# The passage between two layers of a graph network: where the last chunk but one accumulates, when its h is taken, and when the self weights are loaded

## What is computed

```python
def _layer(h, e_h, src, dst, iso_mask, norm, W_r, W_sl, W_el):
    self_msg = jnp.where(iso_mask[:, None], h @ W_el, h @ W_sl)
    msg = (e_h + h[src]) @ W_r
    agg = segment_sum(msg, dst, num_segments=h.shape[0])
    return rrelu(agg * norm + self_msg)

h = relu(layernorm(x))
for W_r, W_sl, W_el in [(W_r1, W_sl1, W_el1), (W_r2, W_sl2, W_el2)]:
    h = _layer(h, e_h, src, dst, iso_mask, norm, W_r, W_sl, W_el)
x = x + h          # then a second layernorm, qk = h @ Wqk, and attention along the edges
```

## Time and profile before

| | |
|---|---|
| runs | 801.25 us median of 3 (798.9 to 801.87) |
| profiled execution | 801.75 us, its span 800.0 us |
| PE busy | 721.3 us (90%) |
| DVE, ACT, POOL busy | 515.8, 430.2, 239.1 us |
| chain that ended last | PE 68%, DVE 9%, DMA 7%, ACT 6%, issue 6% |
| mean granted clock of PE | 0.925 |

### The profile page before, as it was taken

One profiled execution on the slowest core, in us unless ns is written; L12 is line 12 of the kernel. 1 busy time (PEld: TensorE's weight loads), 2 busy tenths in 40 slices (PEclk: granted clock), 3 DMA queues, 4 the chain that ended last, 5 costly groups with the idle time before them and its releaser, 6 DMA issues.

```text
span 800.0 us, 15458 instructions
## 1 busy us (share of the span) xinstructions
PE 721.3 (90%) x5799; PEld 537.1 (67%) x5799; DVE 515.8 (64%) x932; ACT 430.2 (54%) x1085; POOL 239.1 (30%) x272
## 2 busy tenths in 40 slices
PE   3566699989899999988999999899999999999995
PEld 2545588879899998877988999544444444444455
DVE  5798999978788777441333333433665757565667
ACT  0557566756466656562111111477676767677671
POOL 7200000000000222210000000256665766666663
PEclk6555589999999999999999999999999999999997
DMA  4102000032310000101222111210000000000000
GB/s 131 45 7 60 17 2 8 13 104 71 98 45 8 8 8 8 43 30 56 65 87 75 38 38 35 89 47 0 1 15 12 13 13 14 13 14 13 4 24 20
DMA packets 39763, 27.89 MB, mean 35 GB/s; under 512 B 5311, under 2 KB 38163, under 8 KB 39686
## 3 DMA queue, kind: packets, MB, share of 16 engines
q1 hardware_dynamic: 38514, 25.89, 11.2%
q10 hardware_dynamic: 1172, 0.98, 0.4%
HBM read 13.28 MB, written 10.80 MB: 30 GB/s over the span
## 4 chain that ended last, share of the span: by engine, by line
PE 68%; DVE 9%; DMA 7%; ACT 6%; issue 6%; SPq 2%; ACTq 1%; POOL 1%; POOLq 0%; DVEq 0%
PE sums L1492 16%; PE sums L1475 15%; PE sums L1013 12%; PE sums L1086 8%; PE sums L1052 8%; DVE work L842 2%; ACT counts L1268 2%; DMA h_attention<-work 2%; DMA work<-in_x 2%; SPq L554 2%; DVE work L836 2%; PE sums L1020 1%; DMA counts<-in_x 1%; PE sums L1109 1%; PE sums L1027 1%
## 5 line engine op out<-in xcount | busy, mean ns | idle before, releaser
L1571 POOL TENSOR_TENSOR counts<-counts,work 125x500 f32<-125x500 f32 x150 | 165.4, 1102 | 95.5 <-DVE work L1632 88.4
L1052 PE MATMUL sums<-work 125*128 125x196 f16 (+15 forms) x1220 | 154.9, 253 | 20.4 <-DVE work L842 20.3
L1632 DVE SCALAR_TENSOR_TENSOR work<-sums,counts 125x500 f32<-125x500 f32 x150 | 101.7, 678 | 105.4 <-ACT sums L1589 105.4
L1492 PE MATMUL sums<-work 125*128 125x500 f32 (+1 forms) x350 | 159.0, 544 | 7.5 <-DVE work L1632 4.5
L1475 PE MATMUL sums<-work 128*125 128x500 f32 x300 | 150.5, 583 | 0.0
L1584 ACT ACTIVATE sums<-sums,work 125x500 f32<-125x500 f32 (+1 forms) x157 | 102.0, 650 | 75.3 <-PE sums L1475 72.0
L836 DVE TENSOR_TENSOR work<-work,counts 125x3024 f16<-125x3024 f16 (+1 forms) x60 | 114.3, 1905 | 35.9 <-PE sums L1054 32.5
L1268 ACT CAST counts<-sums 128x364 f32 (+38 forms) x305 | 131.3, 471 | 2.5 <-issue 0.6
L1054 PE MATMUL sums<-work 125*128 125x10 f16 (+15 forms) x800 | 132.0, 194 | 0.0
L842 DVE TENSOR_TENSOR work<-work,counts 125x4200 f16<-125x4200 f16 (+15 forms) x120 | 125.5, 1085 | 0.0
L1013 PE MATMUL sums<-counts 125*128 125x250 f16 (+1 forms) x975 | 121.6, 269 | 3.4 <-ACT work L1200 3.2
(11 more groups left out here) (177 smaller groups left out, 687.7 us busy)
## 6 DMA issues: line engine op xcount, KB each, us to landing
first_columns<-counts SPq DMA_DIRECT2D x5, 610.4 KB
counts<-first_columns SPq DMA_DIRECT2D x5, 610.4 KB
counts<-counts SPq DMA_DIRECT2D x5, 468.8 KB
counts<-in_x SPq DMA_DIRECT2D x5, 312.5 KB
h_nodes<-counts SPq DMA_DIRECT2D x5, 312.5 KB
work<-in_x SPq DMA_DIRECT2D x12, 125.0 KB
x_after_messages<-work SPq DMA_DIRECT2D x12, 125.0 KB
h_attention<-work SPq DMA_DIRECT2D x12, 125.0 KB
```

Of the source, the lines that this page charges most:

```text
L1052: pe.matmul(win[:, 0:c, cols], lo[:, k * 2 * LO:k * 2 * LO + 128], m[:, k, h0 * w:(h0 + c) * w].rearrange("p (h d) -> p h d", d=w), start= ...
L1492: last = pe.matmul(ps_o[c % 2][:, 0:cols(u) // n], h3[:, source(c, j + i), :], pbuf[u % PB][:, i * NP:i * NP + cols(u) // n], start=j + i ...
L1571: pool.tensor_tensor(a, a, p, ALU.add).then_inc(acc_done, 1)
L1632: dve.scalar_tensor_tensor(pbuf[u % PB], ps_s[u % 4][0:NP, 0:WIDE], float(np.exp(-CLIP)), counts[0:NP, source(c, j), target(c) * WIDE:(tar ...
```

## The change

Three edits.

1. Chunk 11 accumulates in banks 4 and 5 (those of group 197) in place of 2 and 3 (those of group 199). PE's own 11 waits for `put` of 2 * 198, which is groups 0 to 197, and no longer for all 200 groups.
2. ACT's own 11 stands ahead of the drain of group 199, and no longer behind it.
3. The two halves of `ws` are issued on ACT behind rest 12, ahead of split 6 and the branch. `wr` stays behind the branch and behind `agg_done`, and ACT first waits there until both halves of `ws` have landed. PE waits for `ws` alone ahead of layer two's first self matmuls, and for `wr` behind them.

The other lines belong to the second path, which the flag skips for these inputs: it must leave the self weights of layer one or two in place when it has run.

```diff
-    banks1 = lambda c: (psum[:, 2, :], psum[:, 3, :]) if c == DIRECT + 1 else (psum[:, 6, :], psum[:, 7, :])
+    banks1 = lambda c: (psum[:, 4, :], psum[:, 5, :]) if c == DIRECT + 1 else (psum[:, 6, :], psum[:, 7, :])
...
-                    pe.wait_ge(put, 2 * READY[c] if c <= DIRECT else 2 * GROUPS)
+                    pe.wait_ge(put, 2 * max(READY[c], GROUPS - 2) if c == DIRECT + 1 else 2 * READY[c])
...
             def weigh(i, c):
                 if i == 0:
-                    pe.wait_ge(L["wts"], 16 * 3)
+                    pe.wait_ge(L["wts"], 16 * 2)
                 pe.wait_ge(L["turned_out"], i + 1)
...
                 last.then_inc(L["self"], 1)
+                if i == 0:
+                    pe.wait_ge(L["wts"], 16 * 3)
                 pe.wait_ge(L["summed_out"], i + 1)
...
                     if kind in ("own", "self", "rest"):
                         layer1(kind, q)
+                if g == GROUPS - 1:
+                    layer1("own", DIRECT + 1)
                 c = reach(g)
...
-            layer1("own", DIRECT + 1)
             split(0, 0)
...
             layer1("rest", LAST)
+            for t, v in zip((ws[:, 0:D], ws[:, D:]), weights2[1:]):
+                act.dma_start(t, v).then_inc(L["wts"], 16)
             split(6, 0)
...
             act.wait_ge(agg_done, CHUNKS)
-            for t, v in zip((wr, ws[:, 0:D], ws[:, D:]), weights2):
-                act.dma_start(t, v).then_inc(L["wts"], 16)
+            act.wait_ge(L["wts"], 16 * 2)
+            act.dma_start(wr, weights2[0]).then_inc(L["wts"], 16)
```

More of the change, by code:

```diff
@@ L384, in again_sp @@
         sp.dma_start(hn[0:NP, :], h_dram).then_inc(R["hn_in"], 16)
+        sp.wait_ge(L["wts"], 16 * 2)
+        for t, v in zip((ws[:, 0:D], ws[:, D:]), weights1[1:]):
+            sp.dma_start(t, v).then_inc(R["edges"], 16)
     def again_pool(pool):
@@ L467, in again_dve @@
         dve.memset(zeros_r, 0.0).then_inc(R["begin"], 1)
-        dve.wait_ge(R["edges"], 48)
+        dve.wait_ge(R["edges"], 80)
         dve.wait_ge(R["ramp"], 1)
@@ L598, in _ @@
                 sp.dma_start(heads.rearrange("p (j d) -> p j d", d=HEAD), counts[0:NP, 0:NB, 0:HEAD]).then_inc(R["heads"], 16)
-                sp.wait_ge(R["heads"], 16)
+                for t, v in zip((ws[:, 0:D], ws[:, D:]), weights2[1:]):
+                    sp.dma_start(t, v).then_inc(R["heads"], 16)
+                sp.wait_ge(R["heads"], 48)
             sp.wait_ge(put, 2 * GROUPS)
@@ L1137, in _ @@
                 again_pe(pe)
+                pe.wait_ge(R["heads"], 48)
                 own(0, ORDER2[0])
```

## The result

| | before | changed |
|---|---|---|
| median of 11 runs | 801.87 us (798.75 to 807.9) | 795.57 us (790.71 to 797.56) |
| profiled execution | 801.75 us | 796.59 us |
| its span | 800.0 us | 794.8 us |

The ratio is 0.9912, 95% interval 0.989 to 0.9934: 5.3 to 8.8 us faster; the two medians are 6.3 us apart. The forecast was 794.0 with a range of 791.5 to 797.8, faster by more than 0.5% with a chance of 0.85.

A forecast was written before the change was run, and what follows sets the result against it. The prediction took PE, running with no gap ahead of the passage and from layer two on, as the bound. 2.0 + 1.7 + 2.2 + 1.9 = 7.8 us off 801.75 gave 794.0 us, range 791.5 to 797.8.

The forecast's parts named there:

- the 75 sums start earlier: Chunk 11's sums on PE start at 343.2 in place of 345.19: 2.0 us won, bounds 1.6 to 2.1.
- they run at full clock: Chunk 11's 75 sums no longer run at the lower clock: 1.7 us won, bounds 0 and 1.8.
- the branch's idle: PE's idle from 366.8 to 368.45, at the branch over the second path, was counted as the branch's and unchanged.
- L1109 without its wait: PE's wait for the last weight half ahead of L1109 goes: 2.2 us won, bounds 0.3 and 2.25.
- first round at full clock: Layer two's first round, L1109 to L1099, no longer runs at the lower clock: 1.9 us won, bounds 0 and 1.9.
- The first place: Around own 11, edits 1 and 2: sums start 2.0 us earlier and run 1.7 us faster at full clock.
- The second place: Ahead of L1109, edit 3: 2.2 us of idle go and the first round gains 1.9 us at full clock.
- the clause on contention: Weight DMAs took 2.7, 3.6 and 5.8 us to land because SP's loads of x and `first_columns` run beside them.
- The rule against the row: A compare-and-branch takes about 108 ns by the skill, so some 1.5 us of PE's idle there would be no branch.
- The rivals: Clock falls all the same (0.18), a wait turns into another (0.10), change does not do what it says (0.04), slower (0.03).
- The store of h for attention: Its landing should precede the next load of x: slack 3.4 us against 2.9 us; if not, up to 1.5 us return.
- the third rival: Own 11 still starts late because of a wait hidden behind the drain; 4.1 of 7.8 us left, 797.9; chance 0.04.

The follow-up runs named there:

- e3: Kernel before with only chunk 11's banks and PE's shorter wait changed; ACT's order and the weight loads as before: 801.18 us, ratio 0.9972.
- e4: Kernel before with 25 unused matmuls added ahead of own 11 and 20 ahead of layer two's first weigh: 800.34 us, ratio 0.9962.
- e7: Kernel before, with SP holding back its first large load of `first_columns` until layer two's three weights have landed: 798.91 us, ratio 0.996.
- e5: Changed kernel without PE's branch and PE's part of the second path: 792.28 us, ratio 0.9881.
- e6: Changed kernel with turned h of chunks 11 and 12 in their second bank, sums not waiting for ACT's copy, agg behind the first sums: 790.77 us.
- e8: The changed kernel, unedited, timed and profiled once more on another chip: 792.37 us, ratio 0.9897.
- e10: Changed kernel without the weight-load lines that the change adds to SP's unused second path: 797.12 us, ratio 0.9906.
- e9: Kernel before plus only the weight-load lines that the change adds to SP's unused second path: 802.03 us, ratio 0.9973.
- e1: Changed kernel with the weight loads put back as before, keeping the new banks and ACT's order: 799.28 us, ratio 0.9961.
- e2: Kernel before with only the earlier loading of the two `ws` halves; banks and own 11 as before: 796.19 us, ratio 0.9929.

## Why the prediction was right, and where it was off

By its own steps, from before's profile to the changed one's, in the order of the passage:

| step | forecast, us | measured, us |
|---|---|---|
| the 75 sums start earlier | 2.0 | 2.16 |
| they run at full clock | 1.7 | 1.67 |
| the branch's idle | 0 | 0.34 |
| L1109 without its wait | 2.2 | 2.41 |
| first round at full clock | 1.9 | 1.77 |
| sum | 7.8 | 8.35 |

- The first place. The mechanism and both sizes held; the sums started 0.2 us earlier than forecast. e3 splits it into banks and order, e4 splits the clock off: the waits and the clock are two effects, and each was about half of the gain (2.16 and 1.67 us).
- The second place. It held, and the clause on contention can be made exact: e7 shows 2.3 of the 5.8 us as the large load's share.
- The rule against the row. e5 decides for the row: without the branch and the block that it skips the idle is gone. The compare-and-branch itself may take what the Trainium skill says (Advanced Engine Details and Errata, Control Flow Timing); what stands around it on PE here is 1.30 to 1.82 us in the eleven profiles with the branch. By the rule some 1.2 us of the changed kernel's 1.32 would have been left in e5 (an estimate: 1.32 less the 108 ns that the Trainium skill gives there). How the idle divides between the branch and getting behind the skipped block, no run shows.
- The rivals. No fall of the clock was seen in the passage of the changed kernel, of e5, e6, e8 or e10. No wait took the place of another. The store of h for attention was in time: the next load of x was issued 0.10 us behind the turn's end (384.55 against 384.24 + 0.21).
- What was missed. First, 0.92 us in rounds of layer two that I had taken as unchanged. The prediction has the chain of before run through PE with no gap from layer two on. Its own rows do not say that: at 395.44 the chain stands in a DMA, the store of h, and read in full it runs through SP's loads and stores and what stands between them from 388.8 to 433.8 us. In the changed kernel's profile the chain from the first turn to 440 us is PE's. So some microseconds of the old chain were not PE's, and 0.92 of them went; the cause is not settled (e9, e10). Second, the stretch ahead of the passage, which I had allowed a fall more or less: it went from 339.3 to 344.9 us over twelve profiles. The changed kernel's own profile has it 4.07 later than before's, which ate nearly half of the gain there. Its median, 1.6 over the forecast, is one over such executions.
- How much was luck. That the median came within 1.6 us of 794.0 is in part luck, since two misses of opposite sign met. The passage and the rounds gave 1.5 us more than forecast, the stretch ahead took 4.07. With that stretch as in before the changed profile would have had 792.5, and e8's, which has it 0.6 shorter than before's, has 791.98: both inside the range of 791.5 to 797.8, near its lower end.
- Two slips in the prediction's sums, neither of which moves the forecast. For the store issued at 384.13 with traffic until 386.5 the landing is 2.4 us, not 2.9. And with 4.1 us left of the gain the third rival's time is 797.65, not 797.9.
- What does not quite close. Passage and rounds together give 9.3 us in the profiles, the medians 5.3 to 8.8 us, and e8's ratio 4.8 to 11.7. A part could be executions of before in which the clock did not fall in the passage; no profile shows one.

## What to carry to other kernels

Price an idle stretch of PE twice: the stretch, and the slower matmuls behind it where the granted clock falls; here the waits gave back 4.57 us and the faster matmuls 3.44, and 45 useless matmuls in the gaps showed that the two are separate. When one engine's in-order queue stands between two others, look at which of its steps is needed last, and put it behind the others. Cut two profiles at events that both have, before reading medians that differ by less than their runs; then read the chain in each piece, also in the pieces that the change doesn't touch.

## What the runs showed of the hardware

- A fall of the clock does not follow from the length of the idle stretch alone. In the passage it fell in or behind 1.96, 2.25, 2.32, 2.62 and 3.07 us (e3, before, e1, e3, before). At the stretch near 163.5 us, with the same instructions around it, it fell with 2.29, 3.21 and 3.27 us of idle (e7, e3, e5) and stayed with 2.32, 2.33, 3.21 and 3.27 (before, e8, e6, e10). The shortest stretch with a fall behind it was 1.84 us, near 210 us (e2, e4). Behind the branch's 1.30 to 1.82 us it never fell, in eleven profiles.
- At the lower level the 75 sums' stretch cost 1.67 us for 3.4 us of it, and a longer stretch (e2, 0.53 in the mean from 342.1 to 349.3) 2.6: 0.72 ahead of the sums and 1.86 in them.
- Leaving out a branch together with the long block that it always skips made the passage 1.5 us shorter on PE (e5). Four DMAs that never run, in a skipped block of SP's, went with a stop of 0.37 us between two of SP's issues: it was there in all six profiles without them and in none of the six with them.
